# A four-layer graph network on one core: ScalarE's order of work and the clearing of the sum buffer between passes

## The reference, cut to what matters

```
h = relu(layernorm(x)); x = x + L0(h)   # relational: h @ w[type16], times edge weight, summed by target
h = relu(layernorm(x)); x = x + L1(h)   # Chebyshev, K = 3: two propagations of w_hat * v[src], summed by target
h = relu(layernorm(x)); x = x + L2(h)   # attention over 86 edge types, relu
h = relu(layernorm(x)); x = x + L3(h)   # mean of h[src] over the edges of each target
```

## Time and profile before

| | us |
|---|---|
| median of 3 runs | 8780.03 (8773.54 to 8781.4) |
| the profiled execution, its own time | 8783.14 |
| its span, first to last instruction | 8781.2 |
| busy: POOL, PE, PEld, DVE, ACT | 6340.0, 5476.9, 4260.2, 4149.4, 2474.1 |

### The profile page before, as it was taken

One profiled execution on the slowest core, in us unless ns is written; L12 is line 12 of the kernel. 1 busy time (PEld: TensorE's weight loads), 2 busy tenths in 40 slices (PEclk: granted clock), 3 DMA queues, 4 the chain that ended last, 5 costly groups with the idle time before them and its releaser, 6 DMA issues.

```text
span 8781.2 us, 148222 instructions
## 1 busy us (share of the span) xinstructions
PE 5476.9 (62%) x36704; PEld 4260.2 (49%) x36705; DVE 4149.4 (47%) x13145; ACT 2474.1 (28%) x7662; POOL 6340.0 (72%) x6409
## 2 busy tenths in 40 slices
PE   3333333333377767677777777777777777776777
PEld 1222222232366656344444444466666666665666
DVE  2555555565677776222222222233344334437886
ACT  3444444444222221222222222211111111112221
POOL 0777777777577775777777777677777777765775
PEclk9555555555566776555555555555555555557887
DMA  9100000000122223233333333311111111113332
GB/s 153 14 14 14 14 14 14 14 14 14 31 51 50 51 49 46 90 114 112 112 112 112 112 116 108 113 39 38 38 38 38 39 38 38 39 34 71 86 85 64
DMA packets 563918, 515.64 MB, mean 59 GB/s; under 512 B 358580, under 2 KB 498900, under 8 KB 538580
## 3 DMA queue, kind: packets, MB, share of 16 engines
q1 hardware_dynamic: 358756, 350.87, 13.2%
q0 software_dynamic: 204912, 162.46, 11.6%
HBM read 266.21 MB, written 246.66 MB: 58 GB/s over the span
## 4 chain that ended last, share of the span: by engine, by line
POOL 55%; issue 23%; DVE 8%; PE 7%; DVEq 3%; DMA 2%; SPq 1%; POOLq 1%; ACT 0%; ACTq 0%
POOL arena L617 55%; DVE tbuf L1546 4%; PE ps_agg L942 2%; DVE tbuf L1540 2%; PE ps_t L1065 2%; DMA arena<-nodes,ibuf 1%; SPq L483 1%; PE ps_wide L1052 1%; DMA arena<-table,ibuf 1%; DMA table<-tbuf 1%; DVE msg L1566 1%; PE ps_t L1201 1%; DVEq L1563 0%; PE ps_h L1201 0%; DVEq L449 0%
## 5 line engine op out<-in xcount | busy, mean ns | idle before, releaser
L617 POOL DMA_INDIRECT arena<-table,ibuf x3328 | 3269.8, 983 | 1169.1 <-issue 1045.4
L617 POOL DMA_INDIRECT arena<-nodes,ibuf x3072 | 3067.6, 999 | 1139.3 <-issue 915.8
L942 PE MATMUL ps_agg<-mem_a,arena 128*32 128x80 f32 (+1 forms) x4736 | 641.9, 323 | 777.9 <-DVEq L1309 772.8
L942 PE MATMUL ps_agg<-mem_b,arena 128*32 128x80 f32 (+1 forms) x4736 | 596.6, 308 | 695.5 <-DVEq L1309 683.4
L942 PEld LDWEIGHTS ps_agg<-mem_a,arena 128*32 128x32 f32 (+1 forms) x4736 | 563.0, 165 | 872.1 <-DVEq L1309 807.7
L1121 PE MATMUL ps_wide<-w2f,ht 33*128 33x462 f32 (+1 forms) x1372 | 973.0, 899 | 0.0
L942 PEld LDWEIGHTS ps_agg<-mem_b,arena 128*32 128x32 f32 (+1 forms) x4736 | 520.3, 155 | 775.1 <-DVEq L1309 732.0
L1332 DVE TENSOR_TENSOR big<-big,ps_agg 32x80 f32 (+1 forms) x592 | 138.5, 234 | 1398.7 <-PE ps_agg L942 1347.1
L1121 PEld LDWEIGHTS ps_wide<-w2f,ht 33*128 33x128 f32 x1372 | 440.8, 330 | 550.5 <-issue 508.0
L1546 DVE TENSOR_SCALAR tbuf<-iota,at_f 128x256 bf16<-128x256 bf16 x2940 | 647.1, 299 | 10.1 <-issue 10.1
L1141 PE MATMUL ps_agg<-tbuf,msg 128*64 128x80 f32 x2496 | 373.5, 344 | 419.1 <-DVE msg L1694 419.1
(11 more groups left out here) (325 smaller groups left out, 9203.6 us busy)
## 6 DMA issues: line engine op xcount, KB each, us to landing
table<-tbuf SPq DMA_DIRECT2D x98, 1089.0 KB, 4.2
table<-tbuf SPq DMA_DIRECT2D x98, 1039.5 KB
idx_a<-lows_d SPq DMA_DIRECT2D x300, 192.0 KB
arena<-table,ibuf POOLq DMA_INDIRECT x3328, 2.5
arena<-nodes,ibuf POOLq DMA_INDIRECT x3072
table<-tbuf SPq DMA_DIRECT2D x25, 1024.0 KB, 4.4
tbuf<-lows_d SPq DMA_DIRECT2D x120, 192.0 KB
idx_a<-lows_d SPq DMA_DIRECT2D x60, 224.0 KB
```

What stands on the lines that cost most here:

```text
L617: nc.gpsimd.indirect_dma_start(out=INTO[s][:, k, c, 0:WIDTH[s]], out_offset=None, in_=TABLE[s], in_offset=bass.IndirectOffsetOnAxis(ap=ibu ...
L942: last = nc.tensor.matmul(ps_agg[ROW0[s]:ROW0[s] + CHN[s], 0:WIN], narrow[:, k, c, 0:CHN[s]], onehots[b][:, c, :], start=(c == 0), stop=(c ...
```

## The change

Three things are moved.

1. `lay_out_first` for passes 1 and 4 goes ahead of `split_rows` in ScalarE's program.
2. The memset of `big` ahead of passes 1 and 4 leaves VectorE. ScalarE writes the zeros, one block behind each transposed block, inside `norm_blocks`: seven copies from a column of zeros, 1,792 elements each and 2,048 the last, in 128 partitions (pass 1) or 96 (pass 4). A drain closes them.
3. The store of the nodes for pass 2 goes ahead of the load of the 86 types on SyncE.

```diff
+        zero = sb("zero", [P, 1])
...
             sp.wait_ge(sums[1]["all_added"], 1)
+            store_nodes(1, 1, lambda i: ubuf[1][i])
             edge_array(idx_a, et86, s_et86)
-            store_nodes(1, 1, lambda i: ubuf[1][i])
...
+            def clear_turned(n, i, rows):
+                act.wait_ge(s_turned, TURNED[0 if n == 1 else 3] + i + 1)
+                at = slice(i * BT * P, SW if i == NB - 1 else (i + 1) * BT * P)
+                nc.scalar.copy(big[0:rows, at], zero[0:rows, 0:1].to_broadcast([rows, at.stop - at.start]))
+
             def norm_blocks(n, width):
                 for i in range(NB + 1):
                     if i < NB:
                         square(n, i)
                     if i > 0:
                         root(n, i - 1, width)
+                        if n == 1:
+                            clear_turned(n, i - 1, P)
+                        if n == 3:
+                            clear_turned(n, i - 1, SPLIT)
+                if n > 0:
+                    act.drain()
...
             def pick_and_lay_out(s, h):
-                lay_out_first(s)
...
             norm_blocks(1, 2)
+            lay_out_first(1)
             split_rows(0, 0, lambda i: ubuf[0][i])
...
             norm_blocks(3, 1)
+            lay_out_first(4)
             split_rows(1, 3, lambda i: cols(H, i, D))
...
             def clear_sums(s):
                 dve.sem_inc(s_free, SLOTS)
-                rows = [2 * D, P, 0, 2 * D, SPLIT][s]
+                rows = [2 * D, 0, 0, 2 * D, 0][s]
...
+            V.memset(zero[:, :], 0.0)
```

## The result

| | before | after |
|---|---|---|
| median of 7 runs, us | 8777.94 (8773.54 to 8781.4) | 8747.21 (8743.29 to 8751.08) |
| ratio, 95% interval | | 0.9965 [0.9955, 0.9975] |
| the profiled execution | 8783.14 | 8743.33 |

The change makes the kernel faster by 0.35%, 30.7 us between the medians; the interval of the ratio spans 22 to 40 us. So passes and transitions are compared each for itself.

The account below looks back on a forecast made before the run. GpSimd's gathers were taken to bound passes 1 and 4, so its earlier start counts: 16.6 + 17.0 + 0 for the types = 33.6 us, taking the median from 8780.0 to 8746.4, range 8738 to 8762.

Parts of the forecast that it names:

- What releases the first gather: Ahead of passes 1 and 4: the last node store, not ScalarE's row numbers; first gather 17.2 and 17.7 us earlier.
- The clears: Seven ScalarE copies of zeros per pass, at most 2.1 us each, the last 2.4; all but the last hidden in the norm.
- It has 14.4 us of waits for gathers in the pass to give. It does.: Pass 1: VectorE starts 13.4 us earlier, not 17.2, and makes up the 3.8 us from its waits for gathers.
- The term was 16.6: Pass 1's gain: 17.2 us from the earlier first gather less 0.6 for gathers slowed beside the split.
- the rival that only the memset counts: VectorE is the bound and only its memset counts: 2 x 13.4 = 26.8 us gained, 8753; chance 0.09.
- the chain's links to VectorE there: Pass 1: the chain steps to VectorE for some 700 us; the prediction trusted GpSimd's row without gaps above 0.3 us instead.
- Pass 4: the term was 17.0: Pass 4's gain: 17.7 us from the earlier first gather less 0.7 for slowed gathers, GpSimd not held up.
- the 2.1 us of the forecast: Near pass 4's end: distance from an add to the next gather into its slot, 6.4 us less 4.3; GpSimd needs 0.94.
- Gathers beside the split: Early gathers of passes 1 and 4 slowed beside the split: 0.6 us in pass 1, 0.7 in pass 4.
- the forecast's nearer row: Gathers beside the split's second subtraction lost 0.55 us a pass; about five at 0.3 each make 1.5, 1.0 more.
- its worst case: Worst slowing of an early gather in pass 2 applied beside the split: 0.5 us for each of seven, 3.5 us.
- The types: Pass 2: types at 3524, first slot free at 3533, needed at 3548.45; cost 0, at worst 1.5 us.

Follow-up runs that it names:

- rows_alone3: Kernel before with only the row numbers moved ahead of the splitting, VectorE keeping its memset; 8768.43 us, ratio 0.999.
- types_thrice: Changed kernel with the 86 edge types loaded three times over behind the node stores, each load waiting for the one before; 8768.73 us, ratio 0.9982.
- two_slots_first: Changed kernel, GpSimd gathering only two groups ahead in passes 1 and 4 until the first group is added; 8757.15 us, ratio 0.997.
- few_gathers: Changed kernel, GpSimd gathering only the first 128 of each group's 1,024 rows in pass 1; 8719.41 us, ratio 0.9927.
- types_alone: Kernel before with only the types' load moved behind the node stores, on a slower chip (before: 11,170.78 us); 11170.56 us, ratio 1.0.

## Why the prediction was right, and where a term was off

The forecast was 8746.4 and the median is 8747.21; gain forecast 33.6, measured 30.7. By the parts:

- **What releases the first gather**: right in both passes, in time (17.2 and 17.3 us sooner; forecast 17.2 and 17.7) and in kind (a store).
- **The clears**: right and inside the bound (1.67 and 1.88 us against at most 2.1 and 2.4), hidden in the norm, whose last block ended 48.7 us behind pass 0's last gather in both kernels. Pass 4's row numbers did not have to wait.
- **Pass 1: the step that failed is "It has 14.4 us of waits for gathers in the pass to give. It does."** The term was 16.6. The pass ended 12.1 to 12.8 us sooner (1158.9 and 1158.2 against 1171.0), and its successor started 12.8 to 13.3 us sooner. That is about what VectorE gained by its memset, 13.4, and not the 16.6 that GpSimd's start was to give. rows_alone3 shows it pure: with GpSimd 17 us ahead and VectorE where it was, nothing is gained; and from rows_alone3 to after, where the memset goes too, the end moves by 12.8 us. The 14.4 us weren't a reserve. What VectorE doesn't wait for gathers at the end of a turn, it waits for TensorE's product there. Both waits together are 58.8 us before, and 63.2, 60.6, 64.7 and 62.9 in after, types_thrice, two_slots_first and rows_alone3, however they are shared out. In types_thrice GpSimd was the slower one: its gathers took 1.322 us each and not the 1.316 of after, it lost 4.0 of its 17.2 us by the last gather, and the pass still ended within 0.7 us of after's. So the two are level, and for pass 1 the rival that only the memset counts was right on the size; the chain's links to VectorE there, which I set aside, pointed the right way.
- **Pass 4: the term was 17.0.** The program's end, from pass 3's last gather, came 19.8 us sooner in after, 17.7 in types_thrice and 14.5 in few_gathers. Here GpSimd sets the end: it starts 17.3 us sooner, never stands still, and the end follows its last gather by 52.9 us. Its slots were never as tight as the 2.1 us of the forecast: 7.9 us at the least in after and 3.8 in types_thrice, against 6.4 before. What differs from 17.3 is how long the gathers themselves took, 593.8 to 599.1 us against 596.3 before. rows_alone3 gains 11.8 us in this pass without touching VectorE.
- **Gathers beside the split**: forecast 0.6 us a pass. The first 16 gathers of pass 1 took 22.2 us and not 21.0, the first 32 took 43.0 and not 41.3: 1.2 to 1.7 us. That is between the forecast's nearer row (1.0 more) and its worst case (3.5), nearer the row. In pass 4 the first 32 took 42.4 against 42.9: nothing.
- **The types**: 0 forecast, no gap in GpSimd's row measured, and the price of lateness as forecast at the one delay that was tried.

Two parts, 12.8 + 17.7, make 30.5 in types_thrice; 13.3 + 19.8 make 33.1 in after's profile; the medians say 30.7. That the total came so near is in part luck: the change moves GpSimd by 17.2 us and VectorE by 13.4, so a forecast for pass 1 that went by the wrong one of the two was off by only 3.3 to 3.8 us, less than the medians can resolve. Pass 4 was right by its mechanism. The profile's own difference of 39.9 us has 5.8 us more from pass 2 and 1.8 from pass 3. Pass 2's gathers took 2134.5 us in the profile of before and 2128.7 in after, but also 2128.3 in rows_alone3, whose pass 2 is that of before: the one profile of before was slow there.

What stays open: VectorE's first block of pass 1 was added 15.1 us sooner in after and types_thrice (13.4 from the memset, the rest because it no longer waited for the first gathers), its last only 12.1 and 12.8. The 2.3 to 3.0 us went in 25 turns, which took 42.34 and 42.31 us each and not 42.22. TensorE's clock in those turns was 0.70 before and 0.68 in both; whether that makes the difference wasn't tried.

None of the complete versions has a lower ratio than the changed kernel's 0.9965 at 8,750 us (few_gathers leaves work out); two_slots_first's 0.997 can't be told from it.

## What to carry to other kernels

A gap-free row proves that an engine never waited, not that the stage ends when it ends: when two engines are level, both look like the bound, and an edit that moves one of them is paid only up to what the other moves. Before a wait is counted as reserve, see what would be waited for in its place. Compare the distance from the last gather to the last add, before and after: it shows in one number whether one of two engines has run ahead for nothing. Take it from more than one execution: the same pass 1 gave 13.2 us in after and 6.8 in types_thrice. And move one engine by itself, as rows_alone3 does: when an edit moves both by nearly the same, the total can't say which of them counted.

## What the runs showed of the hardware that was not expected

**Gathers and one-input instructions.** Beside gathers, VectorE's 128x256 bf16 one-hot instruction took 306 ns in the mean and up to 496; without them 279 and at most 295. This is 0.3 us of the 1.38 by which a turn of the loop is longer beside gathers (40.96 us without, 42.2 to 42.3 with them); with VectorE's other instructions it is 0.7, and the rest is waiting for TensorE. So the loop that is faster than GpSimd by itself was as slow as GpSimd beside it.

**The same program at 11,170 and 11,430 us.** On two other chips the kernel before took 27% and 30% longer, in all of its 33 and 35 runs there. In the profile a gather still took 0.94 us where nothing disturbed it, and the granted clock over the span was 0.57 against 0.59; what was different is TensorE's "issue" time. The timeline of TensorE in the first turn of pass 1 (types_alone), at the end of the first 32 gathers (2956.6 to 2996.8) and behind them:

```profile
2993.30 0.37 PE L1065 MATMUL ps_t<-tbuf,mem_a 128*96 128x256 bf16 x1 [2.43 <-issue]
2995.40 0.37 PE L1065 MATMUL ps_t<-tbuf,mem_a 128*96 128x256 bf16 x1 [1.73 <-issue]
2998.20 0.37 PE L1065 MATMUL ps_t<-tbuf,mem_a 128*96 128x256 bf16 x1 [2.43 <-issue]
...
3001.70 0.88 PE L1049 MATMUL ps_wide<-arena,tbuf 128*128 128x32 bf16 x26 [0.49 <-issue]
```

From 2983.5 to 2998.2 TensorE began one matmul every 1.4 to 2.8 us, and then, 5 us behind the end of the last gather, 26 in 0.9 us, while GpSimd stood still for want of a slot. Over pass 1 of that run TensorE began 5.4 matmuls a us while GpSimd gathered and 9.1 in its pauses; on the first chip 10.1 beside the gathers. It may be that GpSimd's early start pays in another way there, because what it gathers beside the splitting is out of TensorE's way later; that is argued from the traces and was not tested, and what lies behind the slow issue no run here shows.

**ScalarE writes zeros** at 0.9 ns an element and partition (1.67 us for 1,792, 1.88 for 2,048), the same in 96 and in 128 partitions.
